# Causal convolution: three VectorE passes replaced by four diagonal matrices on TensorE

## The reference

```
xr, z = split(xm @ W_in)                    # [512, 1024] each, per batch
xt = causal depthwise conv(xr, W_conv, K=4) # xt[c,t] = sum_k W_conv[c,k] * xr[c, t-3+k]
u = silu(xt + b_conv)
dt, Bm, Cm = split(u @ W_x, [64, 16, 16]);  delta = softplus(dt @ W_dt + b_dt)
h[t] = exp(delta[t]*A) * h[t-1] + delta[t]*u[t]*Bm[t]   # 16 states per channel
y = sum_n h[t,n]*Cm[t,n] + u*D;  y = y * silu(z);  out = y @ W_out
```

## Time and profile before

| | us |
|---|---|
| median of 3 runs | 4128.2 (4123.81 to 4128.88) |
| the profiled execution | 4128.04 |
| its span | 4126.2 |
| `setup` ends, `mix` begins | 74.5, 1804.5 |
| first scan | 1896.5 |

### The profile page before, as it was taken

The page is one execution under the profiler, slowest core; times in us unless marked ns, Lnnn a source line. Parts: engine busy times, 40 slices in busy tenths (PEclk is TensorE's granted clock), DMA queues, the critical chain, the costliest instruction groups (busy, mean ns, idle before and its releaser), DMA issues.

```text
span 4126.2 us, 36124 instructions
## 1 busy us (share of the span) xinstructions
PE 3383.7 (82%) x12298; PEld 1802.2 (44%) x12298; DVE 2844.3 (69%) x3658; ACT 1906.8 (46%) x3262; POOL 1901.7 (46%) x1139
## 2 busy tenths in 40 slices
PE   5798989898989898876688878878888788788857
PEld 1444444444444444334444444444444454444443
DVE  1344444444444444336999999999999999999993
ACT  0232222232222222227467676775676766756742
POOL 0021212121212121207677677786776867767771
PEclk8899999999999999996689979989899799898958
DMA  5001000000000000101121212222212122221110
GB/s 209 33 0 38 7 31 13 27 17 21 24 21 23 21 23 21 51 30 44 39 90 62 95 61 85 71 67 92 91 62 96 64 79 72 69 105 67 44 54 21
DMA packets 99799, 220.85 MB, mean 54 GB/s; under 512 B 10577, under 2 KB 10689, under 8 KB 97569
## 3 DMA queue, kind: packets, MB, share of 16 engines
q1 hardware_dynamic: 95904, 211.06, 15.1%
q10 hardware_dynamic: 3712, 7.47, 0.5%
HBM read 184.67 MB, written 33.83 MB: 53 GB/s over the span
## 4 chain that ended last, share of the span: by engine, by line
POOL 17%; issue 13%; PE 13%; DVE 10%; ACT 3%; DMA 0%; POOLq 0%; SPq 0%; DVEq 0%
POOL HS L1110 12%; PE bank L1461 10%; DVE HS L1340 5%; DVE acc L1345 4%; PE bank L1478 3%; POOL delta L1125 1%; POOL DU L1128 1%; POOL ZS L1116 1%; ACT bank L1187 1%; DVE U L1377 1%; POOL comb L1141 1%; POOL DU L1119 0%; PE bank L1487 0%; POOL comb L1144 0%; DVE G L1365 0%
## 5 line engine op out<-in xcount | busy, mean ns | idle before, releaser
L1110 POOL TENSOR_TENSOR HS<-DU,brep 128x1024 f32<-128x1024 f32 x512 | 1197.0, 2357 | 539.7 <-PE bank L1478 539.7
L1340 DVE TENSOR_TENSOR_SCAN HS<-bank,HS 128x1024 f32<-128x1024 f32 x512 | 1166.6, 2279 | 74.5 <-ACT bank L1187 61.8
L1478 PE MATMUL bank<-ident,HS 128*128 128x128 f32 x4096 | 696.2, 322 | 375.6 <-DVE acc L1345 342.2
L1187 ACT ACTIVATE bank<-delta,aneg 128x511 f32<-128x511 f32 x1024 | 661.7, 680 | 535.5 <-DVE HS L1340 533.0
L1478 PEld LDWEIGHTS bank<-ident,HS 128*128 128x128 f32 x4096 | 565.0, 166 | 647.9 <-DVE HS L1340 435.9
L1345 DVE SCALAR_TENSOR_TENSOR acc<-bank,C,acc 128x512 f32<-128x512 f32 x960 | 665.1, 733 | 40.4 <-PE bank L1478 39.6
L431 POOL TENSOR_TENSOR PR<-PR,rrec 128x512 f32<-128x512 f32 x256 | 261.6, 1043 | 894.9 <-DVE rrec L665 894.9
L1461 PE MATMUL bank<-XM,w_l 128*128 128x512 f32 x1024 | 502.4, 638 | 43.8 <-DVE U L1377 18.9
L1461 PE MATMUL bank<-w_l,G 128*128 128x512 f32 x1024 | 473.5, 608 | 9.4 <-ACT delta L1197 3.9
L520 ACT ACTIVATE PR<-bank,nsmax 128x512 f32<-128x512 f32 x256 | 173.7, 683 | 449.4 <-DVE nsmax L661 449.4
L715 PE MATMUL bank<-w_l,NT 128*128 128x512 f32 x768 | 358.5, 612 | 0.9 <-ACT NT L487 0.9
(11 more groups left out here) (164 smaller groups left out, 3740.5 us busy)
## 6 DMA issues: line engine op xcount, KB each, us to landing
brep<-b_d SPq DMA_DIRECT2D x256, 256.0 KB, 3.2
w_l<-in_L_cond_W_in SPq DMA_DIRECT2D x14, 2048.0 KB, 9.6
w_l<-in_L_cond_W_out SPq DMA_DIRECT2D x7, 2048.0 KB, 9.1
w_l<-in_L_cond_W_full SPq DMA_DIRECT2D x7, 2048.0 KB, 9.3
X<-in_x SPq DMA_DIRECT2D x8, 1024.0 KB, 7.6
x_d<-X SPq DMA_DIRECT2D x8, 1024.0 KB, 4.3
xm_d<-XM SPq DMA_DIRECT2D x8, 1024.0 KB, 3.9
attn_d<-PR SPq DMA_DIRECT2D x8, 1024.0 KB, 5.6
```

The lines of the kernel that those rows point to most:

```text
L1110: nc.gpsimd.tensor_tensor(HS[:, u % DEEP], DU[:, chunks(j, s), :], brep[:, m % 3, :].unsqueeze(1).to_broadcast([P, UC, T]), ALU.mult).then ...
L1187: last = nc.scalar.activation(dA[:, s, i, 1:T], delta[:, c, 1:T], ACT.Exp, scale=aneg[:, c, n:n + 1])
L1340: nc.vector.tensor_tensor_scan(h, dA[:, u % 2].rearrange("p i t -> p (i t)"), h, 0.0, ALU.mult, ALU.add).then_inc(scanned, 1)
L1478: last = nc.tensor.transpose(y_bank[t % 2][:, i * P:(i + 1) * P], h, ident[:])
```

## The change

`setup` makes for each of the 8 channel blocks and 4 taps a 128x128 matrix with the tap's weights on its diagonal (GpSimd, identity times the weight column), 2 MB in all, and SP stores them in DRAM as `diag_d`, in two parts of 4 blocks. In `mix` ScalarE copies each xr bank to a staging row of 515 columns with three zeros ahead (`stage`, three rows that take turns, in the memory of `e_abs`), and TensorE multiplies four shifted views of 512 columns with the four diagonal matrices into another ring bank (`cv`). ScalarE then writes `U` from it with the bias alone. The ring has 8 more uses per batch. The diagonal matrices have no memory of their own: for each batch SP reloads them into two of the three slots of `ZS` (`load_diag`, 1 MB each, at slot 19 of the half before and at slot 1), and z overwrites them. GpSimd zeroes the three pads again for each batch. The tables shift: most items of the front from z on stand one slot or more later, and the silu and output of the tail four slots earlier.

```diff
+                for q in range(2):
+                    sp.wait_ge(diag_done, (q + 1) * IC // 2 * TAPS)
+                    sp.dma_start(diag_d[q], diag[:, q * IC // 2:(q + 1) * IC // 2]).then_inc(diag_out, 16)
                 sp.wait_ge(gate_out, 16)
+                sp.wait_ge(diag_out, 2 * 16)
...
+                for c in range(IC):
+                    for k in range(TAPS):
+                        nc.gpsimd.tensor_tensor(diag[:, c, k, :], ident[:], convw[:, c, k:k + 1].to_broadcast([P, P]), ALU.mult).then_inc(diag_done, 1)
...
         PE_XR = {0: 0, 1: 1, 2: 2, 4: 3, 5: 4, 6: 5, 8: 6, 9: 7}
-        PE_Z = {10: 0, 11: 1, 14: 2, 20: 3, 22: 4, 23: 5, 25: 6, 26: 7}
-        PE_XD = {12: 0, 13: 1}
-        PE_DT1, PE_C = {15: 0, 16: 1, 18: 2, 19: 3}, 17
+        PE_CV = {2: 0, 3: 1, 4: 2, 6: 3, 7: 4, 8: 5, 10: 6, 11: 7}
+        PE_Z = {12: 0, 13: 1, 15: 2, 21: 3, 22: 4, 23: 5, 25: 6, 26: 7}
+        PE_XD = {13: 0, 14: 1}
+        PE_DT1, PE_C = {16: 0, 17: 1, 19: 2, 20: 3}, 18
...
-        ACT_CONV0 = {0: 0, 3: 1, 4: 2, 6: 3, 7: 4, 8: 5, 10: 6, 11: 7}
-        ACT_SILU_U = {9: (0, 1, 2, 3), 13: (4, 5, 6, 7)}
-        ACT_Z = {12: 0, 14: 1, 16: 2, 23: 3, 25: 4, 26: 5, 28: 6, 29: 7}
-        ACT_A1, ACT_LN1 = {17: 0, 18: 1, 21: 2, 22: 3}, {20: (0, 1), 24: (2, 3)}
-        ACT_OUT = {36: (0, 1, 2, 3)}
-        DVE_CONV = {1: 0, 2: 1, 3: 2, 5: 3, 6: 4, 7: 5, 9: 6, 10: 7}
-        DVE_XD, DVE_C = 14, 18
-        POOL_CORR1, POOL_DELTA1 = {20: 0, 22: 1, 24: 2, 26: 3}, {21: 0, 23: 1, 25: 2, 27: 3}
-        POOL_OUT = {37: 0, 38: 1, 39: 2, 40: 3}
+        ACT_XR = {1: 0, 2: 1, 3: 2, 5: 3, 6: 4, 7: 5, 9: 6, 10: 7}
+        ACT_CV = {3: 0, 4: 1, 5: 2, 7: 3, 8: 4, 9: 5, 11: 6, 12: 7}
+        ACT_SILU_U = {10: (0, 1, 2, 3), 13: (4, 5, 6, 7)}
+        ACT_Z = {14: 0, 15: 1, 17: 2, 24: 3, 25: 4, 26: 5, 28: 6, 29: 7}
+        ACT_A1, ACT_LN1 = {18: 0, 19: 1, 22: 2, 23: 3}, {21: (0, 1), 25: (2, 3)}
+        ACT_OUT = {32: (0, 1, 2, 3)}
+        DVE_XD, DVE_C = 15, 19
+        POOL_CORR1, POOL_DELTA1 = {21: 0, 23: 1, 25: 2, 27: 3}, {22: 0, 24: 1, 26: 2, 28: 3}
+        POOL_OUT = {33: 0, 34: 1, 35: 2, 36: 3}
+        SP_XR, SP_Z, SP_D0, SP_D1, POOL_PADS = 24, 2, 19, 1, 19
...
+                def load_diag(n, q):
+                    if q == 0:
+                        after(sp, corr_done, n * IC)
+                    else:
+                        after(sp, g_done, (2 * n - 1) * HC)
+                    sp.dma_start(ZS[:, (2 * n + q) % 3], diag_d[q].rearrange("p c k m -> p c (k m)")).then_inc(diag_in[q], 16)
...
                 load_xm(0)
+                load_diag(0, 0)
+                load_diag(0, 1)
...
+                def pads(n):
+                    pool.wait_ge(corr_done, n * IC)
+                    nc.gpsimd.memset(e_flat[:, 0:3 * LONG].rearrange("p (i t) -> p i t", t=LONG)[:, :, 0:TAPS - 1], 0.0).then_inc(pads_zero, 1)
...
-                        nc.scalar.activation(U[:, c, :], ring.bank(n, f"xr{c}")[:], ACT.Identity, scale=convw[:, c, TAPS - 1:TAPS],
-                                             bias=col("L1_cond_b_conv", c)).then_inc(conv0, 1)
+                        nc.scalar.activation(U[:, c, :], ring.bank(n, f"cv{c}")[:], ACT.Identity, bias=col("L1_cond_b_conv", c)).then_inc(
+                            ring.emptied["act"], 1)
+                    if s in ACT_XR:
+                        c = ACT_XR[s]
+                        act.wait_ge(ring.full, ring.at(n, f"xr{c}"))
+                        if c == 0:
+                            after(act, corr_done, n * IC)
+                        if c >= 3:
+                            act.wait_ge(ring.full, ring.at(n, f"cv{c - 3}"))
+                        nc.scalar.activation(stage(c)[:, TAPS - 1:LONG], ring.bank(n, f"xr{c}")[:], ACT.Identity).then_inc(ring.emptied["act"], 1)
...
-                        for k in range(TAPS - 1):
-                            lag = TAPS - 1 - k
-                            y = U[:, c, lag:T]
-                            last = nc.vector.scalar_tensor_tensor(out=y, in0=ring.bank(n, f"xr{c}")[:, 0:T - lag], scalar=convw[:, c, k:k + 1],
-                                                                  in1=y, op0=ALU.mult, op1=ALU.add)
...
+                    if s in PE_CV:
+                        c = PE_CV[s]
+                        if c % HC == 0:
+                            pe.wait_ge(diag_in[c // HC], (n + 1) * 16)
+                        if c == 0:
+                            pe.wait_ge(pads_zero, n + 1)
+                        ring.wait_free(pe, n, f"cv{c}")
+                        pe.wait_ge(*ring.done(n, f"xr{c}"))
+                        product(ring.bank(n, f"cv{c}")[:], lambda k: diag(n, c)[:, k, :], lambda k: stage(c)[:, k:k + T],
+                                range(TAPS), TAPS).then_inc(ring.full, 1)
```

More of the change, by code:

```diff
@@ L153, in build, with setup @@
             X = sb("X", [P, TT, D], c=early)
[L154 removed]
+            setup(nc, a, bank, ident, cols, bq8, aneg, convw, per_batch, gate_d, diag_d, X, load, arrived)
             attend(nc, a, bank, ident, cols, col, bq8, per_batch, x1_d, xm_d, attn_d, X, W, load, load_wide, arrived)
[L156 to L159 removed]
+        mix(nc, a, out, space, bank, ident, col, aneg, convw, x1_d, xm_d, attn_d, gate_d, b_d, diag_d, wide, load_wide, arrived)
+def setup(nc, a, bank, ident, cols, bq8, aneg, convw, per_batch, gate_d, diag_d, X, load, arrived):
     ctx = ExitStack()
@@ L870, in _, with mix @@
                 l1(B - 1, None)
-def mix(nc, a, out, space, bank, ident, col, aneg, convw, x1_d, xm_d, attn_d, gate_d, b_d, wide, load_wide, arrived):
+def mix(nc, a, out, space, bank, ident, col, aneg, convw, x1_d, xm_d, attn_d, gate_d, b_d, diag_d, wide, load_wide, arrived):
     ctx = ExitStack()
@@ L910, in mix @@
         b_out = sem("b_out")
-        conv0, u_done = sem("conv0"), sem("u_done")
+        u_done, diag_in, pads_zero = sem("u_done"), [sem(f"diag_in{q}") for q in range(2)], sem("pads_zero")
         sp_abs, sp_exp, sp_w, sp_w1, sp_ln = sem("sp_abs"), sem("sp_exp"), sem("sp_w"), sem("sp_w1"), sem("sp_ln")
@@ L994, in chunks, with stage, diag @@
             return slice(c, c + UC)
+        e_flat = e_abs[:].rearrange("p c t -> p (c t)")
+        LONG = T + TAPS - 1
+        def stage(c):
+            return e_flat[:, c % 3 * LONG:(c % 3 + 1) * LONG]
+        def diag(n, c):
+            return ZS[:, (2 * n + c // HC) % 3, c % HC, :].rearrange("p (k m) -> p k m", m=P)
         def zs(n, c):
@@ L1053, in half0 @@
                             weights("full", b, "z7")
+                        if b + 1 < B and s == SP_D0:
+                            load_diag(b + 1, 0)
                         if b + 1 < B and s == SP_XM:
@@ L1067, in half1 @@
                             front(n, s)
+                            if s == SP_D1:
+                                load_diag(n, 1)
                             if s == SP_OUT:
@@ L1152, in half0 @@
                             finish_delta(b, POOL_DELTA0[s])
+                        if s == POOL_PADS and b + 1 < B:
+                            pads(b + 1)
                         if p is not None:
@@ L1234, in front @@
                         for c in ACT_SILU_U[s]:
-                            act.wait_ge(*ring.done(n, f"xr{c}"))
+                            act.wait_ge(*ring.done(n, f"cv{c}"))
                             nc.scalar.activation(U[:, c, :], U[:, c, :], ACT.Silu).then_inc(u_done, 1)
                         act.preload_act_table_set(EXP_AND_LN)
-                    if s in ACT_CONV0:
-                        c = ACT_CONV0[s]
-                        act.wait_ge(ring.full, ring.at(n, f"xr{c}"))
+                    if s in ACT_CV:
+                        c = ACT_CV[s]
+                        act.wait_ge(ring.full, ring.at(n, f"cv{c}"))
                         after(act, du_done, (n - 1) * IC + c + 1)
@@ L1251, in front @@
                         after(act, g_done, (2 * n + c // HC - 2) * HC)
+                        if c % HC == 0:
+                            act.wait_ge(ring.full, ring.at(n, f"cv{c + HC - 1}"))
                         if c >= HC:
@@ L1367, in front @@
                 def front(n, s):
[L1368 to L1373, removed]
-                        for k in range(TAPS - 1):
-                            lag = TAPS - 1 - k
-                            y = U[:, c, lag:T]
-                            last = nc.vector.scalar_tensor_tensor(out=y, in0=ring.bank(n, f"xr{c}")[:, 0:T - lag], scalar=convw[:, c, k:k + 1],
-                                                                  in1=y, op0=ALU.mult, op1=ALU.add)
-                            if k < TAPS - 2:
-                                link_front(last)
-                        last.then_inc(ring.emptied["dve"], 1)
                     if s == DVE_XD:
```

14 lines of the change are left out of this document (9 added, 5 removed).

## The result

The changed kernel takes 4248.6 us (median of 4 runs, 4247.0 to 4252.7), the kernel before 4127.3 beside it; the ratio is 1.0297, interval 1.0279 to 1.0314. It is slower by 121 us, and the forecast was 4249. The profiled executions differ by 4247.0 - 4128.0 = 119.0 us. Parts of the sum were wrong in both directions, though, and seven of the nine forecasts of the experiments got the size wrong.

The account below looks back on a forecast made before the run. VectorE was taken to set the pace in the second halves before the change. Seven second halves 84.7, batch 0's front 25.4, loads 7 and setup 4 summed to 121.1 us on 4128.0, giving 4249; range 4189 to 4316.

Parts of the forecast that it names:

- Slots 1 to 15: Early slots of a second half: TensorE sets every slot with 20 products, +13.5 us on 68.5.
- The test put first: Second halves: TensorE work beyond 1.5 us of lateness in one slot isn't taken up by free time later.
- Slots 16 to 31: Later slots of a second half: -1.5 us for VectorE caught up, +1.6 for z products, -1.5 for GpSimd's stall.
- The first halves: First halves of the batches: no part of the change lies there, 0.
- Before the scans: Everything ahead of the first scan, setup, loads and batch 0's front: 36 us more.
- Setup: Setup's end: SP stores 2 MB of diagonal blocks and waits for it, +4 us (0 to 8).
- loads ahead of w_x: Start of the last stage: 2 MB of diagonal blocks queued before w_x delay TensorE, 7 us (6 to 10).
- the front: Batch 0 before the scans, on TensorE alone: +27.4 us of products less 1.99 of z0's wait, +25.4.
- (1): Second halves: VectorE's relief wins, each shrinks by 17.8 us, total 4039; chance 0.07.
- (2): Slots 1 to 15: ScalarE empties banks late in most, 0.8 us each, 12 more per half, 4333; chance 0.13.
- (3): TensorE products at the skill page's price, 1.7 us for four matmuls, total some 4150; chance 0.03.
- (4): Whole kernel: TensorE's extra work falls into what VectorE gives up, all cancels within 0.2%; chance 0.02.

Follow-up runs that it names:

- e8: Changed kernel with VectorE's three passes per block done again, reading the projection's ring bank and releasing it in ScalarE's place; 4275.25 us, ratio 1.0359.
- e1: Changed kernel with batch 0's eight blocks kept on VectorE, its two diagonal loads ahead of w_x gone; 4223.35 us, ratio 1.0236.
- e3: Changed kernel without the reloads of the diagonal blocks for batches 1 to 7; 4249.94 us, ratio 1.0300.
- e9: Kernel before with blocks 1, 4 and 6 convolved by TensorE, batch 0 all on VectorE, z's blocks from the second on later; 4104.22 us, ratio 0.9943.
- e7: Kernel before with blocks 1 and 4 convolved by TensorE, batch 0 all on VectorE, the changed kernel's earlier tail kept; 4107.64 us, ratio 0.9952.
- e5: Changed kernel with VectorE also doing 24 passes per batch on SBUF scratch, result unused; 4305.47 us, ratio 1.0427.
- e6: Changed kernel with blocks 1 to 7 of z moved to slots 21 to 30; 4230.89 us, ratio 1.0248.
- e2: Changed kernel with one matmul in place of four per convolution product, three taps left out; 4119.11 us, ratio 0.9982.
- e4: Kernel before with one of the three VectorE passes per block, two taps left out; 4078.19 us, ratio 0.9883.

## Why the prediction was right, and where it was only lucky

**Slots 1 to 15: right.** From xr1's start to slot 16's transposes 81.83 us (2344.93 to 2426.76) against 82.0 forecast. Its terms stand one by one: one first product of 4.04 us (4.16), all others 3.43, transposes 0.88, xd's wait 0.24 (0.4). Granted clock 0.98, no fall. The test put first, that TensorE's extra work isn't taken up by free time in later slots, is what the row of 4.00 us of VectorE idling shows, and in e8 17.8 us of passes put back into a half lengthen it by 3.5: VectorE's load has all but ceased to set these slots.

**Slots 16 to 31: right.** The half shown grew from 140.36 to 152.28 us, 11.9 against 12.1: slots 1 to 15 gave 13.35, the stretch ahead of xr1 0.3, so the rest gave -1.7, forecast -1.4. z3 to z5 stand at 4.3 us as forecast (idle 2.63, then 0.70 and 0.70); GpSimd's stall shrank from 1.28 to 0.77 us and didn't vanish. The mean of the seven is lower, 11.3, for another reason: the third, fifth and seventh take 150.6 us and not 152.2 to 153.1. They differ in the opening alone: xr1 starts 1.0 us sooner and takes 3.44 us instead of 4.04, at a granted clock of 1.00 (2630.70 to 2634.50) against 0.86 (2345.00 to 2349.00); what stands behind slot 16's transposes lasts 62.0 us in both kinds. The forecast had no term for that.

**The first halves: wrong.** Forecast 0, measured +9.1. The step that failed is "The first halves and the last second half have no part of the change: 0", in its first part (the last second half took 114.3 us before and after). They take either about 132.3 us, as before, or 134.6 to 135.2, and after the change four of the seven behind batch 0's are of the longer kind. TensorE in a long one (from 2489 us) and in a short one (from 2774 us), the same two products of the output:

```profile
2497.84 4.55 PE L1498 MATMUL bank<-w_l,G 128*128 128x512 f32 x8
...
2513.35 5.40 PE L1498 MATMUL bank<-w_l,G 128*128 128x512 f32 x8 [0.56 <-ACT delta L1238]
```

```profile
2783.03 3.62 PE L1498 MATMUL bank<-w_l,G 128*128 128x512 f32 x8
...
2797.61 3.70 PE L1498 MATMUL bank<-w_l,G 128*128 128x512 f32 x8 [0.56 <-ACT delta L1238]
```

```profile
2513.00:2517.00 4.00, 3.65 (x5) 1.63 (x6) 3.92 (x7) 3.21 (x6) 4.00 (x2) 0.57 0.19 66
...
2798.00:2801.00 3.00, 3.00 (x8) 1.20 (x7) 3.00 (x3) 2.21 (x5) 3.00 (x2) 1.00 0.20 65
```

Same work, the same wait of 0.56, 0.9 and 1.7 us more, and in the third fence the granted clock in each second product, 0.57 and 1.00: the lower clock falls on other instructions. e1, e3 and e8 (1058.7, 1059.1, 1058.8) have it too, e9 less (1054.8), e7 hardly (1049.8). e5 and e6 have more (1061.7, 1061.3), and e2 and e4 little or none (1050.6, 1046.9). In the changed kernel each long first half stands behind a second half of the long kind (152.2 to 153.1 us). That the long ones come with more load on TensorE in the halves before is read from these sums, and e5, which adds none there, doesn't fit it well; what moves the lower clock was not tested, and the cause stays open.

**Before the scans: the sum is off by 5, by parts of both signs.** Setup +1.8 (76.37 against 74.54; forecast 4, both stores were out after 6.9 us), loads ahead of w_x +4.7 (12.95 us from the stage's begin to the first product, before 8.25; forecast 7), the front +27.5 (forecast 25.4; TensorE's own chain gave 25.3, the rest is a wait for GpSimd's first dbu), and the attention stage, which the change doesn't touch, took 2.8 less (in e1 it took 4.3 more than here, so it moves by that much between executions). The 32 diagonal products took 11.5 us and are hidden.

So 5.9 and 5.1 us too much were balanced by 9.1 us that had no step at all: the forecast sum of 121.1 met 119.0 in the profiled executions and 121.3 in the medians by luck. The total's error is not the error of the reasoning, which is some 5 to 9 us per term.

**The rivals.** (1) falls with the total, by the idling rows and by e8: VectorE's 17.8 us per half were worth something only up to TensorE's floor. e4 measured how far: two of the three passes, 11.9 us, were worth 7.0. The Trainium skill, "Perfetto Trace Analysis", Optimizing Scalar/DVE Operations, says that with a saturated DVE it may make sense to offload some work to ScalarE or even GpSimd; it doesn't speak of TensorE as the receiver, to which the prediction's rival 1 stretched it. Taken that way, with two or three blocks the runs agree (0.9952, 0.9943), with eight they disagree (1.0297): the rule doesn't say how much to move, and the count of free slots gives a first answer. (2) did not happen in the change (0.24 us a half); e8 shows what it costs when it does. (3) falls: 3.43 us for four matmuls, and e2, with a quarter of them, gave back 104 us in the halves, where that rival's price would have had 7 x 10.3 = 72 at most. (4) falls with the total.

## What to carry to other kernels

When two engines hand each other work in every slot through double buffers, price a move slot by slot: a slot lasts as long as its slower engine, and surplus in one slot is not paid by slack in the next. Count the empty places of the receiving engine first, and move only as many pieces as there are such places; here two or three of eight blocks gain 0.5% and all eight lose 3% (four to seven were not tried). Take the slot rule's gains as upper bounds: it forecast 150, 75, 50, 29 and 14 us for e2, e4, e6, e7 and the step to e9, and the runs gave 129, 49, 18, 20 and 3. An engine with idle time can still cost: look for whom its last instruction releases.

## What the runs showed of the hardware that I had not expected

- Three VectorE passes over two SBUF operands took 2.29 us with GpSimd idle and up to 6.14 beside it; with one operand in a bank three stayed at 2.28 to 2.30 in all slots, most of them beside GpSimd (mean 739 ns in e8, 1290 in e5).
- After TensorE had idled 3.06 us (e2) and 1.97 us (e4), the next product took 5.30 us instead of 3.6, at a granted clock of 0.57 in both. In e2 some of what the removed work was worth went back that way.
- First halves with the same instructions differ by 2.3 to 2.9 us with where the lower clock falls; the sum of eight so moved by 9 us (0.2%) without any change in its work, and second halves of one kernel differ by 1.6 us or more in the same way.
